# Per-block scale of the quantised activations: immediates in tensor_scalar against constant columns in tensor_tensor

## The chip, the cores and the metric

The kernel runs on 1 core of one Trainium2 chip. The metric is the device time in microseconds (us) of one execution. The engines are TensorE (PE in the profile), VectorE (DVE), ScalarE (ACT), GpSimd (POOL) and SyncE (SP), which here only issues transfers.

## The reference, cut to what matters

The program computes two layers on x of 8 x 512 x 256 (float32). The first layer, in which the change lies, is a layer norm followed by a state-space block and a quantised feed-forward block, both added to x:

```python
xn = _layernorm(x, axis=-1)
x = x + _L0_attn_ref(xn, ...) + _L0_ffn_ref(xn, w_gate, w_up, w_down)

def fp4_quant_dequant(x):                 # blocks of 16 along the last dim
    scale = jnp.max(jnp.abs(xb), axis=-1, keepdims=True) / 6.0
    scale = jnp.maximum(scale, jnp.float32(1e-12))
    xn = xb / scale
    idx = jnp.searchsorted(_MID, jnp.abs(xn))
    q = _GRID[idx] * jnp.sign(xn) * scale

gate = fp4_linear(x, w_gate); y = fp4_linear(x, w_up)
return fp4_linear(jax.nn.silu(gate) * y, w_down)

def step(h, inp):                         # state-space block, 512 steps
    dA = jnp.exp(d_t[:, :, None] * A[None])
    h = dA * h + (d_t * u_t)[:, :, None] * B_t[:, None, :]
    y_t = jnp.einsum('bdn,bn->bd', h, C_t)
```

The second layer (block-sparse attention, and two rounds of local attention with a feed-forward part) follows and is not touched.

## The kernel before, in words

Four stages run one after the other: the quantisation of the weights (to about 60 us), the state-space stage `mamba_and_fp4_ffn` (about 60 to 1530 us), block-sparse attention, and the local attention layers (from about 2160 us). Each engine has its own program, written out by hand; its order is the order in the code, and semaphores tie the engines together.

In the state-space stage one batch of 512 rows is one iteration, and it has 32 steps s. Each step handles two of the 16 states for 128 of the 512 channels. POOL multiplies `hb` = `bcB` * `du` (L540) for a step; ACT writes the decay `ps_dA` (L780, L782); DVE runs the scan over both (`tensor_tensor_scan`, L633) and multiplies the result by `bcC` into `hb` (L644, semaphore `weighed`); PE adds that into `ps_y` (L988). ACT may write the next but one `ps_dA` only once L644 has read the one before it. Between L633 and L644 of a step DVE runs what else is due in it. POOL works up to 8 steps ahead (a ring of 8 `hb` buffers) and is otherwise held only by its inputs.

The quantisation of activations is cut into three parts (`fp4_part`), placed in three steps in a row. Part 0 finds the largest magnitude of each block (L119), makes `scale` (L120), its reciprocal `inv` (L121), and corrects it by 1 - 2^-24 (L122). Part 1 multiplies by `inv` and makes the rounding constant in `work` (L125 to L127), part 2 rounds by adding and subtracting it (L129, L130). Every instruction of a part but the last waits for the one before it by a semaphore. POOL multiplies by `scale` afterwards (`scale_blocks`, L107).

In one batch part 0 runs five times: for `h` (the hidden rows, 704 values or 44 blocks per partition) in steps 3, 21, 25 and 29, called rows 0, 1, 2 and 3 below (tables `HIDDEN`), and for the next batch's `xn` (1024 values, 64 blocks) in step 13 (`XQ`). That makes 32 and 8 in the whole stage. In steps 1, 2, 4 and 6 PE also sums the output rows of the batch before it.

The stage's constants are set by POOL at its start, and DVE, ACT and PE wait for that count in `s_zero`.

Of the kernel before, what the change touches and what calls it, by code (L numbers as in the profile page):

```python
# [7 lines left out]
ALU = mybir.AluOpType  # L8
# [6 lines left out]
P = 128  # L15
# [54 lines left out]
def bc(ap, shape):  # L70
    return ap.broadcast_to(shape)
# [28 lines left out]
FP4_STEPS = 8  # L100
# [8 lines left out]

def fp4_part(dve, st, rows, blk, work, p, n, part):

    g = n // 16
    amax, scale, inv = blk[0:p, 0, 0:g], blk[0:p, 1, 0:g], blk[0:p, 2, 0:g]
    w = work[0:p, 0:n]
    blocks = rows.rearrange("p (g e) -> p g e", e=16)
    if part == 0:
        st.link(dve.tensor_reduce(amax, blocks, AX.X, ALU.max, apply_absolute_value=True))  # L119
        st.link(dve.tensor_scalar(scale, amax, 1.0 / 6.0, 1e-12, ALU.mult, ALU.max))  # L120
        st.link(dve.reciprocal(inv, scale))  # L121
        return st.done(dve.tensor_scalar(inv, inv, 1.0 - 2.0 ** -24, None, ALU.mult))  # L122
    if part == 1:
        dve.wait_ge(st.s, st.at(st.k))
        st.link(dve.tensor_tensor(blocks, blocks, bc(inv.unsqueeze(2), [p, g, 16]), ALU.mult))  # L125
        st.link(dve.tensor_scalar(w.bitcast(U32), rows.bitcast(U32), EXPONENT, None, ALU.bitwise_and))
        return st.done(dve.tensor_scalar(w, w, 1.0, 1.5 * 2.0 ** 22, ALU.max, ALU.mult))  # L127
    dve.wait_ge(st.s, st.at(st.k))
    st.link(dve.tensor_tensor(rows, rows, w, ALU.add))  # L129
    return dve.tensor_tensor(rows, rows, w, ALU.subtract)  # L130
# [85 lines left out]
def mamba_and_fp4_ffn(nc, io, W, x1_dram, bc_dram, NB):  # L216
# [6 lines left out]
    T, D, DI, NS, R, I = 512, 256, 512, 16, 16, 704  # L223
    TT, DC, IC = T // P, D // P, DI // P
# [11 lines left out]
    HIDDEN = [3, 21, 25, 29]  # L236
# [6 lines left out]
    XQ, TURN_XQ, TAKE_XQ = 13, 30, 31  # L243
# [12 lines left out]
    with ExitStack() as ctx:  # L256
        sb = lambda n, s, d=F32: ctx.enter_context(nc.sbuf_tensor(n, s, d))
        sems = []

        def S(name, per):  # L260
            sems.append(Sem(ctx, nc, name, per))
            return sems[-1]
# [10 lines left out]
        mhalf = sb("mhalf", [P, TT])  # L273
        eps = sb("eps", [P, TT])
        tick = sb("tick", [P, 1])


        xn = sb("xn", [P, TT, D])
# [19 lines left out]
        blk_x = sb("blk_x", [P, 3, TT * D // 16])  # L298
        blk_h = sb("blk_h", [P, 2, 3, I // 16])
        work = sb("work", [P, TT * D])  # L300
# [12 lines left out]
        s_zero = ctx.enter_context(nc.semaphore("a_zeroed"))  # L313
        s_aneg = ctx.enter_context(nc.semaphore("a_negA"))
        x_in = S("a_x_in", 16)
        xr_in = S("a_xr_in", 16)
        x_steps = S("a_x_steps", TT + 1 + FP4_STEPS)
        h_steps = S("a_h_steps", TT * FP4_STEPS)
        mv_ready = S("a_mv", TT)
        g_steps = S("a_g_steps", 2)  # L320
        xn_ready = S("a_xn", TT)
# [57 lines left out]
        def landed(s):  # L379

            return 16 * (s // ROWS + 1)

        def unit(s):
            return divmod(s, GROUPS)
# [88 lines left out]
        def _(pool):  # L473
# [3 lines left out]
            pool.memset(eps[:, :], LN_EPS).then_inc(s_zero, 1)  # L477
            pool.memset(xin[:, :, 0:3], 0.0).then_inc(s_zero, 1)
            pool.memset(nought[:, :], 0.0).then_inc(s_zero, 1)
            pool.wait_ge(s_zero, 6)  # L480

            def prepare(n, s):
                if s == STATS:
# [73 lines left out]
        @block.vector  # L557
        def _(dve):
            xs, hs = Steps(x_steps, dve), Steps(h_steps, dve)
            dve.wait_ge(s_w, 16 * 7)  # L560
            dve.wait_ge(s_zero, 6)
            dve.wait_ge(s_aneg, 1)
            for c in range(IC):
                dve.tensor_scalar(diag_d[:, c, :], W["ident"][:, :], cols[:, 2, c:c + 1], None, ALU.mult)\
                    .then_inc(s_aneg, 1)
                for j in range(4):
                    dve.tensor_scalar(diag_c[:, c, j, :], W["ident"][:, :], conv_w[:, c, j:j + 1], None, ALU.mult)\
                        .then_inc(s_aneg, 1)
            dve.tensor_scalar(a_neg[:, :, :], a_neg[:, :, :], -1.0, None, ALU.mult).then_inc(s_aneg, 1)

            def prepare(n, s):
                if s == STATS:
                    xs.turn(n)

                    dve.wait_ge(x_in.s, x_in.at(n, 16))
                    dve.wait_ge(xn_ready.s, xn_ready.at(n, 0))
                    for t in range(TT):
                        xs.done(dve.bn_stats(stats[:, t, :], xn[:, t, :]))
                    dve.wait_ge(xs.s, xs.at(TT))
                    xs.done(dve.memset(tick[:, :], 0.0))  # L580
                    for t in range(TT):
                        dve.bn_aggr(mv[:, t, :], stats[:, t, :]).then_inc(mv_ready.s, 1)
                if XQ <= s < XQ + 3:
                    rows = xn[:, :, :].rearrange("p t d -> p (t d)")
                    if s == XQ:
                        dve.wait_ge(xn_ready.s, xn_ready.at(n, TT))
                        dve.wait_ge(xn_turned.s, xn_turned.at(n, DC))
                    last = fp4_part(dve, xs, rows, blk_x, work, P, TT * D, s - XQ)
                    if s == XQ + 2:
                        last.then_inc(xg_ready.s, 1)  # L590

            def gate_y(b, c):
                dve.wait_ge(summed.s, summed.at(b, (c + 1) * GROUPS))
                dve.wait_ge(sz_ready.s, sz_ready.at(b, c + 1))
                dve.wait_ge(x1_sum.s, x1_sum.at(b, 0))
                dve.tensor_tensor(y[:, c, :], ps_y[:, :], z[:, c, :], ALU.mult).then_inc(y_ready.s, 1)

            def ffn(b, s, prev):
                for t in range(TT):
                    if HIDDEN[t] <= s < HIDDEN[t] + 3:  # L600
                        rows, blk = h[:, t % 2, :], blk_h[:, t % 2, :, :]
                        if s == HIDDEN[t]:
                            if t == 0:
                                hs.turn(b)
                            dve.wait_ge(sg_ready.s, sg_ready.at(b, t + 1))
                            dve.wait_ge(gated.s, gated.at(b, 2 * t + 2))
                            if t:
                                dve.wait_ge(h_turned.s, h_turned.at(b, 2 * t - 2))
                            elif prev:
                                dve.wait_ge(h_turned.s, h_turned.at(b - 1, 2 * TT - 2))  # L610
                            dve.tensor_tensor(rows.rearrange("p (a n) -> p a n", a=2), ps_p[:, :, 0:HALF],
                                              sg[:, :].rearrange("p (a n) -> p a n", a=2), ALU.mult).then_inc(h_ready.s, 1)
                            dve.wait_ge(h_ready.s, h_ready.at(b, t + 1))
                        last = fp4_part(dve, hs, rows, blk, work, P, I, s - HIDDEN[t])
                        if s == HIDDEN[t] + 2:
                            last.then_inc(hg_ready.s, 1)

            def first(n):
                for s in range(SCANS):
                    prepare(n, s)  # L620

            def tail(b):
                gate_y(b, IC - 1)

            def body(b, prev, more):
                flat = lambda ap: ap.rearrange("p n t -> p (n t)")

                for s in range(SCANS):
                    c, g = unit(s)
                    dve.wait_ge(dA_ready.s, dA_ready.at(b, s + 1))  # L630
                    dve.wait_ge(dBu_ready.s, dBu_ready.at(b, s + 1))
                    tile, h_all = hb[:, s % RING, :, :], dA[:, s % 2, :, :]
                    dve.tensor_tensor_scan(flat(h_all), flat(h_all), flat(tile), 0.0, ALU.mult, ALU.add)\  # L633
                        .then_inc(scanned.s, 1)
                    if g == 0 and c:
                        gate_y(b, c - 1)
                    if s == 0 and prev:
                        gate_y(b - 1, IC - 1)
                    ffn(b, s, prev)
                    if more:  # L640
                        prepare(b + 1, s)
                    dve.wait_ge(scanned.s, scanned.at(b, s + 1))
                    dve.wait_ge(c_in[s % ROWS].s, c_in[s % ROWS].at(b, landed(s)))
                    dve.tensor_tensor(tile, h_all, bcC[:, s % ROWS, :, :], ALU.mult).then_inc(weighed.s, 1)  # L644

            batches(dve, first, body, tail)

        @block.scalar
        def _(act):
            act.wait_ge(s_w, 16 * 7)  # L650
            act.activation(a_neg[:, :, :], a_neg[:, :, :], ACT.Exp).then_inc(s_aneg, 1)
            act.wait_ge(s_aneg, 2 + 5 * IC)
            act.wait_ge(s_zero, 6)

            def softplus(m, c):

# [145 lines left out]
        @block.tensor  # L802
        def _(pe):
            pe.wait_ge(s_w, 16 * 7)
            pe.wait_ge(s_zero, 6)
            pe.wait_ge(s_aneg, 2 + 5 * IC)

            def turn(src, k):
# [1538 lines left out]
```

## Time and profile before

| | us |
|---|---|
| median of 3 runs | 3789.05 |
| lowest, highest | 3785.77, 3795.94 |
| the profiled execution, its time | 3792.24 |
| its span, first to last instruction | 3790.1 |
| state-space stage within it, about | 1470 |
| one batch of that stage in steady state, about | 177 |

Over the whole span PE is busy 87%, DVE 67%, ACT 45%, POOL 42%. These shares mix four stages with different limits, so the state-space stage is read apart from the rest, and in it one steady batch. Times are from the start of the span. A busy span is what the profiler reports for an instruction; where an instruction has been started and cannot go on, that time is inside its duration and not in the idle time before it. So the duration of one instruction of fixed size, at its smallest and at its largest, is the thing to compare.

### The profile page before, as it was taken

To read this page: it belongs to the slowest core of one execution; us is meant where nothing else is said; L and a number is where in the kernel's file an instruction comes from. 1 tells how busy PE (TensorE), PEld (TensorE's weight loads), DVE (VectorE), ACT (ScalarE), POOL (GpSimd) and SP (SyncE) were. 2 spreads that over 40 slices of the span, in tenths; PEclk is the share of its full clock that TensorE was granted. 3 is DMA by queue.
4 is the path that set the end of the run, shared out by engine and by line. 5 is a ranking of instruction groups with operands and counts; after the bars stand their busy time and mean duration, and the time that the engine had idled before them with its cause. 6 is when DMAs were issued, how large, how long until landed. Compare 5 with 4: busy or idle time off the path is not lost. (4 is left out here: it accounts for less than half of the span.)

```text
span 3790.1 us, 50238 instructions
## 1 busy us (share of the span) xinstructions
PE 3296.6 (87%) x16236; PEld 1902.6 (50%) x16236; DVE 2545.5 (67%) x3554; ACT 1706.7 (45%) x4102; POOL 1579.5 (42%) x974
## 2 busy tenths in 40 slices
PE   2788898989798987699999769999999689999998
PEld 1334343444444343466666535655665355656665
DVE  5597989888888889376777545555555255555553
ACT  1564656556473743265566423333333133333332
POOL 1556465655555554000000044444554265555552
PEclk8899999999898998899999979999999799999999
DMA  1565556556565655100110010000000200000000
GB/s 47 192 207 191 198 198 209 200 189 213 181 222 183 208 195 180 53 23 22 33 33 17 28 61 17 17 17 17 17 17 12 69 17 22 22 22 22 22 17 17
DMA packets 146654, 343.30 MB, mean 91 GB/s; under 512 B 14898, under 2 KB 78470, under 8 KB 146582
## 3 DMA queue, kind: packets, MB, share of 16 engines
q1 hardware_dynamic: 138134, 334.02, 26.4%
q10 hardware_dynamic: 8448, 8.39, 0.7%
q8 instruction: 37, 0.61, 0.1%
q14 instruction: 35, 0.29, 0.0%
HBM read 320.87 MB, written 21.50 MB: 90 GB/s over the span
## 5 line engine op out<-in xcount | busy, mean ns | idle before, releaser
L988 PE MATMUL ps_y<-hb,ident 128*128 128x512 f32 x1024 | 537.3, 654 | 160.1 <-DVE hb L644 159.9
L633 DVE TENSOR_TENSOR_SCAN ps_dA<-ps_dA,hb 128x1024 f32<-128x1024 f32 x256 | 585.8, 2288 | 95.7 <-ACT ps_dA L782 65.7
L540 POOL TENSOR_TENSOR hb<-bcB,du 128x1024 f32<-128x1024 f32 x256 | 597.3, 2357 | 22.1 <-DMA bcB<-bc_scratch 14.4
L988 PEld LDWEIGHTS ps_y<-hb,ident 128*128 128x128 f32 x1024 | 194.1, 200 | 430.9 <-DVE hb L644 246.8
L1778 POOL TENSOR_TENSOR c_pr<-c_pr,c_inv 128x512 f32<-128x512 f32 (+1 forms) x256 | 232.6, 935 | 411.5 <-DVE c_inv L1890 409.5
L1348 ACT ACTIVATE b_pr<-b_ps_s,b_negmax 128x256 f32<-128x256 f32 (+1 forms) x512 | 263.8, 527 | 164.7 <-DVE b_negmax L1262 162.9
L2245 PE MATMUL c_ps_s<-c_hT,c_w 128*128 128x512 f32 x704 | 321.0, 603 | 17.2 <-DVE c_hid L1956 15.4
L2007 ACT ACTIVATE c_pr<-c_ps_s,c_negmax 128x256 f32<-128x256 f32 (+1 forms) x512 | 222.2, 446 | 246.4 <-DVE c_negmax L1885 246.4
L782 ACT ACTIVATE ps_dA<-delta,a_neg 128x511 f32<-128x511 f32 x512 | 329.7, 675 | 0.9
L644 DVE TENSOR_TENSOR hb<-ps_dA,bcC 128x1024 f32<-128x1024 f32 x256 | 312.0, 1219 | 5.3 <-issue 0.3
L1755 POOL TENSOR_TENSOR c_q_cos<-c_q_cos,c_q_sin 128x1024 f32<-128x1024 f32 x64 | 150.9, 2358 | 311.3 <-DVE c_q_sin L1864 311.3
L780 ACT ACTIVATE ps_dA<-nought 128x2 f32<-128x2 f32 x256 | 44.2, 173 | 491.3 <-DVE hb L644 490.6
L1262 DVE TENSOR_REDUCE b_negmax<-b_ps_s 128x2 f32<-128x512 f32 (+1 forms) x320 | 204.5, 683 | 71.9 <-PE b_ps_s L1419 70.9
L2095 PE MATMUL c_ps_s<-c_w_qkv,c_xT 128*128 128x512 f32 x512 | 241.1, 615 | 1.4 <-ACT c_xT L1980 1.4
L1885 DVE TENSOR_REDUCE c_negmax<-c_ps_s 128x2 f32<-128x512 f32 (+1 forms) x256 | 147.9, 620 | 127.7 <-PE c_ps_s L2132 127.3
L1206 POOL TENSOR_TENSOR b_xb<-b_xb,b_o_bias 128x1024 f32<-128x1024 f32 x8 | 18.8, 2348 | 497.4 <-DMA b_xb<-x_scratch 497.4
L2245 PEld LDWEIGHTS c_ps_s<-c_hT,c_w 128*128 128x128 f32 x704 | 129.6, 192 | 177.4 <-issue 147.8
L1433 PE MATMUL b_ps_t<-ident,b_pr 128*128 128x128 f32 x1280 | 189.6, 285 | 24.7 <-DVE b_pt L1284 12.8
L1956 DVE SCALAR_TENSOR_TENSOR c_hid<-c_ps_s,c_b_cols,c_gl 128x512 f32<-128x512 f32 x96 | 70.5, 745 | 196.3 <-ACT c_gl L2060 177.0
L1761 POOL TENSOR_TENSOR c_rn<-c_ssc,c_mhalf 128x16 f32<-128x16 f32 x64 | 186.5, 2913 | 31.7 <-DVE c_ssc L1874 31.2
L1433 PEld LDWEIGHTS b_ps_t<-ident,b_pr 128*128 128x128 f32 x1280 | 136.7, 142 | 113.9 <-DVE b_pt L1284 55.7
L1986 ACT ACTIVATE c_sq<-c_ps_s 128x512 f32<-128x512 f32 x128 | 69.5, 594 | 256.3 <-PE c_ps_s L2095 256.3
(234 smaller groups left out, 6405.2 us busy)
## 6 DMA issues: line engine op xcount, KB each, us to landing
bcB<-bc_scratch SPq DMA_DIRECT2D x256, 512.0 KB, 4.8
bcC<-bc_scratch SPq DMA_DIRECT2D x256, 512.0 KB, 4.0
c_x<-stream_scratch SPq DMA_DIRECT2D x16, 512.0 KB, 4.9
c_xr<-stream_scratch SPq DMA_DIRECT2D x16, 512.0 KB, 4.3
xn<-in_x_dram SPq DMA_DIRECT2D x8, 512.0 KB, 5.0
xr<-in_x_dram SPq DMA_DIRECT2D x8, 512.0 KB, 6.2
x_scratch<-xr SPq DMA_DIRECT2D x8, 512.0 KB, 5.2
b_x<-x_scratch SPq DMA_DIRECT2D x8, 512.0 KB, 4.2
```

The source lines that it names most:

```text
L540: pool.tensor_tensor(hb[:, s % RING, :, :], bcB[:, s % ROWS, :, :], bc(du[:, c % 2, :].unsqueeze(1), [P, NG, T]), ALU.mult)\
L633: dve.tensor_tensor_scan(flat(h_all), flat(h_all), flat(tile), 0.0, ALU.mult, ALU.add)\
L644: dve.tensor_tensor(tile, h_all, bcC[:, s % ROWS, :, :], ALU.mult).then_inc(weighed.s, 1)
L782: last = act.activation(dA[:, s % 2, n, 1:], delta[:, c, 1:], ACT.Exp, scale=a_neg[:, c, g * NG + n:g * NG + n + 1])
L988: last = pe.matmul(ps_y[:, :], W["ident"][:, :], hb[:, r % RING, i, :], start=False, stop=(g == GROUPS - 1 and i == NG - 1))
L1262: dve.tensor_reduce(negmax[:, u, 0:heads], ps_s[:, u % 4, :].rearrange("p (h n) -> p h n", h=heads), AX.X, ALU.max, negate=True).then_inc( ...
L1348: last = act.activation(pr[:, u % 8, cols], ps_s[:, u % 4, cols], ACT.Exp, bias=negmax[:, u, i:i + 1], accum_out=den[:, qt, h:h + 1])
L1433: last = pe.transpose(ps_t[:, u % 2, k * P:(k + 1) * P], pr[:, u % 8, k * P:(k + 1) * P], W["ident"][:, :])
L1778: pool.tensor_tensor(rows, rows, bc(inv[:, u, :].unsqueeze(2), [P, 2, w]), ALU.mult)\
L2007: last = act.activation(pr[:, u % 6, i * w:(i + 1) * w], ps_s[:, u % 4, i * w:(i + 1) * w], ACT.Exp, bias=negmax[:, u, i:i + 1], accum_out ...
L2095: last = pe.matmul(ps_s[:, pair(t) + a, :], xT[:, k, t * P:(t + 1) * P], w_qkv[:, k, a * INNER:(a + 1) * INNER], start=(k == 0), stop=(k = ...
L2245: last = pe.matmul(ps_s[:, pair(j) + a, :], w_1[:, k, at:at + P], hT[:, k, :], start=(k == 0), stop=(k == DC - 1))
```

## The change

In part 0 of `fp4_part` the two `tensor_scalar` instructions become three `tensor_tensor` instructions. The one that did multiply and max with two immediates is split in two, since a `tensor_tensor` does one operation. The second operand is one column of a new tile `cst` (128 x 3), read with step 0 over the 44 or 64 blocks. POOL sets the three columns at the start of the stage. The weights' quantisation (`fp4_steps`) keeps its instructions.

```diff
-def fp4_part(dve, st, rows, blk, work, p, n, part):
+FP4_PART_STEPS = 9
+
+def fp4_part(dve, st, rows, blk, work, cst, p, n, part):
...
     if part == 0:
+        sixth, least, under = (bc(cst[0:p, i:i + 1], [p, g]) for i in range(3))
         st.link(dve.tensor_reduce(amax, blocks, AX.X, ALU.max, apply_absolute_value=True))
-        st.link(dve.tensor_scalar(scale, amax, 1.0 / 6.0, 1e-12, ALU.mult, ALU.max))
+        st.link(dve.tensor_tensor(scale, amax, sixth, ALU.mult))
+        st.link(dve.tensor_tensor(scale, scale, least, ALU.max))
         st.link(dve.reciprocal(inv, scale))
-        return st.done(dve.tensor_scalar(inv, inv, 1.0 - 2.0 ** -24, None, ALU.mult))
+        return st.done(dve.tensor_tensor(inv, inv, under, ALU.mult))
...
+        cst = sb("cst", [P, 3])
...
-            pool.wait_ge(s_zero, 6)
+            for i, value in enumerate((1.0 / 6.0, 1e-12, 1.0 - 2.0 ** -24)):
+                pool.memset(cst[:, i:i + 1], value).then_inc(s_zero, 1)
+            pool.wait_ge(s_zero, 9)
```

On DVE, in step 3 of a batch (row block 0 of `h`), this stood before, with a scan at either end:

```order
L633 SCALAR_TENSOR_TENSOR ps_dA<-ps_dA,hb 128x1024
L611 TENSOR_TENSOR h<-ps_p,sg 128x704
L119 TENSOR_REDUCE blk_h<-h 128x44
L120 TENSOR_SCALAR blk_h<-blk_h 128x44
L121 RECIPROCAL blk_h<-blk_h 128x44
L122 TENSOR_SCALAR blk_h<-blk_h 128x44
L644 TENSOR_TENSOR hb<-ps_dA,bcC 128x1024
```

and this stands there now (the lines are those of the changed kernel):

```order
L642 SCALAR_TENSOR_TENSOR ps_dA<-ps_dA,hb 128x1024
L620 TENSOR_TENSOR h<-ps_p,sg 128x704
L124 TENSOR_REDUCE blk_h<-h 128x44
L125 TENSOR_TENSOR blk_h<-blk_h,cst 128x44
L126 TENSOR_TENSOR blk_h<-blk_h,cst 128x44
L127 RECIPROCAL blk_h<-blk_h 128x44
L128 TENSOR_TENSOR blk_h<-blk_h,cst 128x44
L653 TENSOR_TENSOR hb<-ps_dA,bcC 128x1024
```

Between the reduction and the multiplication by `bcC` there are four instructions in place of three, three of them with two operands in SBUF; nothing else is moved, on DVE or on another engine. The same holds for the other part 0s.

## Rows read from the trace of the kernel before

**Rows 1.** Busy time by window: window, length, engines' busy (instructions), clock, DMA share, GB/s.
```profile
651.00:828.00 177.00, 151.24 (x410) 75.17 (x409) 155.41 (x127) 100.64 (x171) 97.65 (x53) 0.94 0.59 199
```

**Rows 2.** Waits, 651 to 828 us: waiter <- releaser: total us, times, longest.
```profile
PE ps_y L988 <- DVE hb L644: 16.8, 9, 4.6
...
ACT ps_dA L780 <- DVE hb L644: 59.2, 21, 13.4
```

**Rows 3.** Groups by line, DVE: operation, tiles, shapes, count, busy us, mean ns.
```profile
L120 DVE TENSOR_SCALAR blk_h<-blk_h 128x44 f32<-128x44 f32 x32 | 42.2, 1318 | 1.1
...
L122 DVE TENSOR_SCALAR blk_h<-blk_h 128x44 f32<-128x44 f32 x32 | 21.6, 674 | 1.1
...
L122 DVE TENSOR_SCALAR blk_x<-blk_x 128x64 f32<-128x64 f32 x8 | 12.0, 1500 | 0.3
L120 DVE TENSOR_SCALAR blk_x<-blk_x 128x64 f32<-128x64 f32 x8 | 11.8, 1470 | 0.3
```

**Rows 4.** One tile's instructions: duration in ns, smallest/median/largest, first and last start.
```profile
L120 DVE TENSOR_SCALAR blk_h<-blk_h x32: 186/514/5120, 149.6 to 1498.2; 128x44 f32<-128x44 f32 x32
...
L122 DVE TENSOR_SCALAR blk_h<-blk_h x32: 186/187/1803, 150.4 to 1498.9; 128x44 f32<-128x44 f32 x32
L125 DVE TENSOR_TENSOR h<-h,blk_h x32: 867/872/2066, 154.2 to 1502.7; 128x704 f32<-128x704 f32 x32
...
L1874 DVE TENSOR_TENSOR c_ssc<-c_ss,c_tiny x64: 174/651/1383, 2207.3 to 3675.4; 128x16 f32<-128x16 f32 x64
```

**Rows 5.** Timeline, local attention: start, length in us, engine, line, operation, tiles.
```profile
2471.57 1.91 POOL L1768 TENSOR_TENSOR c_qr<-c_q_cos,c_rn 128x1024 f32<-128x1024 f32 x1
...
2472.86 0.65 DVE L1874 TENSOR_TENSOR c_ssc<-c_ss,c_tiny 128x16 f32<-128x16 f32 x1
```

**Rows 6.** Timeline, first batch, step 4: POOL and DVE.
```profile
153.16 2.35 POOL L540 TENSOR_TENSOR hb<-bcB,du 128x1024 f32<-128x1024 f32 x1
...
154.19 2.07 DVE L125 TENSOR_TENSOR h<-h,blk_h 128x704 f32<-128x704 f32 x1
...
155.46 3.00 POOL L540 TENSOR_TENSOR hb<-bcB,du 128x1024 f32<-128x1024 f32 x1
```

**Rows 7.** Timeline, a steady batch, step 3 (row block 0 of h): POOL and DVE.
```profile
668.04 6.96 POOL L540 TENSOR_TENSOR hb<-bcB,du 128x1024 f32<-128x1024 f32 x3
...
669.93 5.12 DVE L120 TENSOR_SCALAR blk_h<-blk_h 128x44 f32<-128x44 f32 x1
...
675.08 0.43 DVE L121 RECIPROCAL blk_h<-blk_h 128x44 f32<-128x44 f32 x1
675.08 1.26 POOL L532 TENSOR_TENSOR du<-delta,u 128x512 f32<-128x512 f32 x1
675.54 0.84 DVE L122 TENSOR_SCALAR blk_h<-blk_h 128x44 f32<-128x44 f32 x1
...
676.58 2.36 POOL L540 TENSOR_TENSOR hb<-bcB,du 128x1024 f32<-128x1024 f32 x1 [0.23 <-POOL du L532]
```

**Rows 8.** Timeline, the same batch, step 13 (xn): POOL and DVE.
```profile
726.25 4.67 POOL L540 TENSOR_TENSOR hb<-bcB,du 128x1024 f32<-128x1024 f32 x2
...
726.99 1.68 DVE L120 TENSOR_SCALAR blk_x<-blk_x 128x64 f32<-128x64 f32 x1
...
728.70 0.55 DVE L121 RECIPROCAL blk_x<-blk_x 128x64 f32<-128x64 f32 x1
...
729.29 1.69 DVE L122 TENSOR_SCALAR blk_x<-blk_x 128x64 f32<-128x64 f32 x1
```

**Rows 9.** Timeline, the same batch, step 25 (row block 2 of h): POOL and DVE.
```profile
786.98 4.65 POOL L540 TENSOR_TENSOR hb<-bcB,du 128x1024 f32<-128x1024 f32 x2
...
788.86 0.52 DVE L120 TENSOR_SCALAR blk_h<-blk_h 128x44 f32<-128x44 f32 x1
...
789.87 1.80 DVE L122 TENSOR_SCALAR blk_h<-blk_h 128x44 f32<-128x44 f32 x1
```

**Rows 10.** Timeline, the same batch: TensorE where it is released late.
```profile
685.07 0.74 PE L952 MATMUL ps_t<-xr,ident 128*128 128x256 f32 x2 [3.59 <-ACT hqT L732]
...
732.16 1.98 PE L988 MATMUL ps_y<-hb,ident 128*128 128x512 f32 x4 [0.31 <-DVE hb L644]
```

More of the change, by code:

```diff
@@ L316, in mamba_and_fp4_ffn @@
         xr_in = S("a_xr_in", 16)
-        x_steps = S("a_x_steps", TT + 1 + FP4_STEPS)
-        h_steps = S("a_h_steps", TT * FP4_STEPS)
+        x_steps = S("a_x_steps", TT + 1 + FP4_PART_STEPS)
+        h_steps = S("a_h_steps", TT * FP4_PART_STEPS)
         mv_ready = S("a_mv", TT)
@@ L560, in _ @@
             dve.wait_ge(s_w, 16 * 7)
-            dve.wait_ge(s_zero, 6)
+            dve.wait_ge(s_zero, 9)
             dve.wait_ge(s_aneg, 1)
@@ L587, in prepare @@
                         dve.wait_ge(xn_turned.s, xn_turned.at(n, DC))
-                    last = fp4_part(dve, xs, rows, blk_x, work, P, TT * D, s - XQ)
+                    last = fp4_part(dve, xs, rows, blk_x, work, cst, P, TT * D, s - XQ)
                     if s == XQ + 2:
@@ L613, in ffn @@
                             dve.wait_ge(h_ready.s, h_ready.at(b, t + 1))
-                        last = fp4_part(dve, hs, rows, blk, work, P, I, s - HIDDEN[t])
+                        last = fp4_part(dve, hs, rows, blk, work, cst, P, I, s - HIDDEN[t])
                         if s == HIDDEN[t] + 2:
@@ L652, in _ @@
             act.wait_ge(s_aneg, 2 + 5 * IC)
-            act.wait_ge(s_zero, 6)
+            act.wait_ge(s_zero, 9)
             def softplus(m, c):
@@ L804, in _ @@
             pe.wait_ge(s_w, 16 * 7)
-            pe.wait_ge(s_zero, 6)
+            pe.wait_ge(s_zero, 9)
             pe.wait_ge(s_aneg, 2 + 5 * IC)
```

## The prediction

> **What bounds the kernel now.** I read the busy time by window first, then the waits, then one steady batch on the timeline.
>
> By window, one steady batch (177 us) has DVE busy 155.4 us and PE 151.2 us, while ACT is at 100.6 and POOL at 97.7 [rows 1]. Two engines are near full, so the question is which is late where. The waits answer it: PE's longest total is 16.8 us for DVE's multiplication L644, and ACT waits 59.2 us for the same instruction [rows 2]. DVE's own order, from scan to scan, is the chain for most steps.
>
> Two places of the batch show how a delay on DVE reaches the others. At 685.07 PE starts a long stretch of work after an idle time of 3.59 us that ends with ACT's copy of `hqT`; that copy stands in ACT's order behind the decay for which ACT waits on L644. From there PE works without a gap of note up to 732.16, where it waits 0.31 us for L644 [rows 10]. So time lost by DVE in step 3 moves the whole PE stretch, and time lost in step 13 is on the path at once. In steps 21, 25 and 29 DVE has no idle time that another engine's own work sets. I therefore count every delay of part 0 in full.
>
> **What is wrong with the two instructions today.** `tensor_scalar` on 44 values takes 186 ns at its smallest and 5120 ns at its largest [rows 4]. The size is always the same, so the rest is waiting inside the instruction. The groups sum to 42.2 + 21.6 + 12.0 + 11.8 = 87.6 us [rows 3]. The timeline names the partner: L120 of 669.93 ends at 675.05, which is when the third of three POOL multiplications ends (668.04 + 6.96 = 675.00), and L122 of 675.54 ends at 676.38, with POOL's L532 (675.08 + 1.26 = 676.34) [rows 7]. DVE and POOL exclude each other here. Everything depends on whether a `tensor_tensor` with both operands in SBUF is excluded too.
>
> **Does tensor_tensor wait as well?** Two kinds of row say yes. In the local attention stage L1874 is a `tensor_tensor` on 16 values with a tile of constants as second operand: it takes 174 ns at its smallest, 1383 at its largest [rows 4]. One of them starts at 2472.86, inside POOL's L1768, and ends at 2473.51; POOL's instruction ends at 2473.48 [rows 5]. In this stage L125, with 704 values, takes 872 ns as a rule and 2066 once [rows 4], at 154.19, inside POOL's L540 that ends at 155.51; and the POOL instruction behind it takes 3.00 us in place of 2.35 [rows 6], so POOL was held in its turn. No row has a two-operand DVE instruction in SBUF running beside a POOL one at its small price. What no row shows is an operand of step 0, a single column; L125's second operand repeats each value 16 times, and that is the nearest.
>
> The Trainium skill says it too, in "SBUF — State Buffer", section "SBUF: two separate sides": the port pair is taken for a whole instruction by a DVE instruction in a two-port mode, or by one with two SBUF inputs against a GpSimd one that reads SBUF. By this rule, which speaks against the change, the sum is the one below; by the view that only two-port modes take the pair it would be that of the first rival. The rows above side with the rule.
>
> **Prices.** Free of POOL, `tensor_tensor` takes 174 ns for 16 values and 872 for 704 [rows 4]: 1.015 ns for each more, so 202 ns for 44 and 223 for 64. Between linked instructions there are 34 ns (675.05 to 675.08, [rows 7]). Where POOL is out of the way, part 0 gets longer by one instruction and its gap (0.24 us) and by 2 x 16 ns: **0.27 us**. A waiting `tensor_tensor` ends about 0.06 us after POOL's for 44 values, 0.08 for 64.
>
> **Part by part, with POOL where it stands today.** The new third instruction matters more by what it meets than by its length.
>
> *Row block 0, step 3* [rows 7]. The first multiplication ends at 675.06, as L120 does. The maximum starts at 675.10, just after POOL's L532 (675.08), and waits till 676.40. The reciprocal (0.43) ends at 676.87. The correction starts at 676.90, inside POOL's next L540 (676.58 + 2.36 = 678.94), and ends at 679.00 in place of 676.38: **2.6 us**. POOL's next instruction waits for DVE, so nothing more follows. The pattern stands in six batches, the second to the seventh (L120 of 3.4 or 5.1 us in each): 15.6 us.
>
> *xn, step 13* [rows 8]. The first ends at 728.67, between two POOL instructions; the maximum starts at 728.70 inside the second, which ends at 726.25 + 4.67 = 730.92, and ends at 731.00. Reciprocal 0.55 and correction 0.22 with their gaps: 731.84, in place of 730.98: 0.87 us, seven times, 6.1 us. (The eighth lies before the first scan; 0.3 at most.)
>
> *Row block 2, step 25* [rows 9]. In the same way the maximum waits from 789.41 to 791.69 (POOL ends at 786.98 + 4.65 = 791.63), and the correction ends at 792.38 in place of 791.67: 0.71 us, seven times, 5.0 us.
>
> *The rest*: L122's median is 187 ns [rows 4], so in most part 0s POOL is idle behind L120. Row blocks 1 and 3 of all batches and 0 and 2 of the last: 18 x 0.27 = 4.9 us. Row block 0 of the first batch: 0 to 2.3 us, since the three instructions of part 1 behind it wait for POOL today and would wait less; I take 1.
>
> *The three memsets* on POOL at the start lie under the loading of the weights: nothing.
>
> The sum is 15.6 + 6.1 + 5.0 + 4.9 + 1.0 = 32.6 us. The profiled execution (span 3790.1, time 3792.24) would go to 3822.7 and 3824.8. Its time is 3.2 us above the median of the runs; on the median the forecast is 3789.05 + 33 = **3822 us**, 0.9% slower.
>
> **The rivals.**
>
> *The new operation does not wait* (its step-0 operand, or its single element per cycle, keeps it off the shared resource). Then 87.6 us [rows 3] become 96 x 0.202 + 24 x 0.223 + 40 x 0.034 = 26.1 us; the gain of 61.5 us gives 3728. For it speaks only that no row has this operand; against it L1874 and L125. 7%.
>
> *DVE slips in between.* The maximum comes 34 ns behind the first multiplication, and may run before POOL's next instruction has really begun. In step 3 the margin is 0.02 us. If it wins there alone, the maximum ends at 675.30, the correction waits for L532 and ends at 676.40 as today, and the sum is 33 - 15.6 = 17, so 3806. 15%. If it wins in steps 13 and 25 too, the later wait swallows the extra instruction there, and only the 18 x 0.27 is left with some tenths: 3794, no change that can be told. Against the second speaks that POOL's instruction had been waiting with its start on record 0.1 us before. 10%.
>
> *The delays are hidden*: PE's stretch from 685 or ACT turns out to be bound by something else than DVE. Then 3789 to 3792. The wait of 0.31 us at 732.16 [rows 10] leaves little room. 6%.
>
> **How the numbers follow.** Forecast 62%, first rival 7%, second 15% and 10%, third 6%. Around the forecast, phases may move: DVE's later times put other part 0s under a POOL instruction (5 of the 18 free ones by 2.36 us would be 12 us more), so the upper end is 3835. The lower end takes in both forms of slipping in and most of the hidden case, and reaches 3790; below it lie the 7% and part of the 6%, above it some 8%. A measurement tells about 0.3%, 11 us, from no change. From the cases: faster 0.07; same 0.10 + 0.06 = 0.16; slower 0.62 + 0.15 = 0.77.
>
> **What would show it.** In the changed kernel's profile the three `blk_h<-blk_h,cst` groups should have smallest durations near 202 ns and largest in the thousands, the maximum and the correction each ending with a POOL instruction. Step 3 should have waits in all three, and a batch should last some 181.5 us in place of 177. If the three groups stand at 0.2 us throughout, the first rival is right, and my reading of L1874 wrong. If the maximum stays at 0.2 us where POOL is busy, DVE slips in. If the waits are there and the batch is not longer, the path was read wrong.

## The result and the profile after

| | time, median of runs (us) | lowest to highest |
|---|---|---|
| before, same chip | 3791.08 | 3785.77 to 3795.94 |
| changed kernel | 3825.58 | 3818.32 to 3827.98 |

The ratio is 1.0088, 95% interval 1.0068 to 1.0108: 34.5 us slower, where the forecast had 33. The profiled execution of the changed kernel is the fastest of its four (3818.32 us, span 3816.4), so its trace shows 26.3 us of the 34.5 against the span of before (3790.1). The other three runs of the changed kernel are 7 to 10 us longer than the profiled one.

From the page of the changed kernel, the busy time of each engine with its share and its count of instructions.

```profile
PE 3297.9 (86%) x16236; PEld 1901.0 (50%) x16236; DVE 2569.5 (67%) x3594; ACT 1705.5 (45%) x4102; POOL 1577.7 (41%) x977
```

DVE has 40 instructions and 24.0 us of busy time more than before (x3554, 2545.5 us). Forty instructions of 0.2 us would be 8 us; most of the rest is waiting inside the three operations. One steady batch and its largest wait of PE, columns as in [rows 1] and [rows 2]:

```profile
671.00:852.00 181.00, 154.19 (x414) 76.89 (x415) 159.25 (x133) 101.01 (x173) 98.64 (x55) 0.93 0.58 197
```

```profile
PE ps_y L997 <- DVE hb L653: 20.2, 10, 5.3
```

DVE is busy 159.2 us of 181 in place of 155.4 of 177, and PE waits 20.2 us for DVE's multiplication (L653 here, L644 before) in place of 16.8. From first scan to last the state-space stage takes 1402.38 us in place of 1372.14: 30.2 more. The rest of the program is 3.9 us shorter in this execution. The block-sparse stage alone, which the change does not touch, takes 614.5 us here and 618.8 in the trace of before, and 614.5 to 625.3 in the traces of the kernels below, so that the time of a single trace differs by some microseconds for this alone.

The new instructions, by tile and line: smallest, median and largest duration in ns, first and last start in us.

```profile
L125 DVE TENSOR_TENSOR blk_h<-blk_h,cst x32: 203/522/5108, 149.0 to 1527.9; 128x44 f32<-128x44 f32 x32
L126 DVE TENSOR_TENSOR blk_h<-blk_h,cst x32: 203/206/2265, 149.3 to 1528.2; 128x44 f32<-128x44 f32 x32
...
L128 DVE TENSOR_TENSOR blk_h<-blk_h,cst x32: 203/203/2076, 150.9 to 1528.9; 128x44 f32<-128x44 f32 x32
```

```profile
L125 DVE TENSOR_TENSOR blk_x<-blk_x,cst x8: 225/1672/1687, 84.0 to 1284.8; 128x64 f32<-128x64 f32 x8
L126 DVE TENSOR_TENSOR blk_x<-blk_x,cst x8: 226/2272/2278, 84.2 to 1286.6; 128x64 f32<-128x64 f32 x8
```

The free prices are 203 and 225 ns (202 and 223 were estimated), the largest are in the thousands: a `tensor_tensor` whose second operand is one repeated column waits for POOL too. Step 3 of one steady batch, DVE and then POOL; it answers to [rows 7]:

```profile
502.11 5.11 DVE L125 TENSOR_TENSOR blk_h<-blk_h,cst 128x44 f32<-128x44 f32 x1
507.25 1.30 DVE L126 TENSOR_TENSOR blk_h<-blk_h,cst 128x44 f32<-128x44 f32 x1
...
509.06 2.07 DVE L128 TENSOR_TENSOR blk_h<-blk_h,cst 128x44 f32<-128x44 f32 x1
```

```profile
500.20 6.95 POOL L549 TENSOR_TENSOR hb<-bcB,du 128x1024 f32<-128x1024 f32 x3
507.23 1.26 POOL L541 TENSOR_TENSOR du<-delta,u 128x512 f32<-128x512 f32 x1
508.73 2.34 POOL L549 TENSOR_TENSOR hb<-bcB,du 128x1024 f32<-128x1024 f32 x1 [0.23 <-POOL du L541]
```

The first multiplication ends with the third of POOL's three (507.22 and 507.15), the maximum with the multiplication of `du` (508.55 and 508.49), the correction with the next one (511.13 and 511.07). All three wait, and the wait of the correction is what makes the 2.6 us of the forecast. Note the start times 507.25 and 507.23: the maximum comes 0.02 us after POOL. Step 13 and step 25 went as written too. The multiplication and the maximum of xn, against [rows 8]:

```profile
561.73 1.67 DVE L125 TENSOR_TENSOR blk_x<-blk_x,cst 128x64 f32<-128x64 f32 x1
563.44 2.27 DVE L126 TENSOR_TENSOR blk_x<-blk_x,cst 128x64 f32<-128x64 f32 x1
```

### The profile page after: what moved, and what is told of

It is laid out like the page before. It is cut to its first block and busy times, and to the rows that moved or that the text cites. A ratio compares the mean times of both kernels' runs of the same rounds, so it can differ in the third digit from the quotient of the medians.

```text
span 3816.4 us, 50503 instructions
## 1 busy us (share of the span) xinstructions
PE 3297.9 (86%) x16236; PEld 1901.0 (50%) x16236; DVE 2569.5 (67%) x3594; ACT 1705.5 (45%) x4102; POOL 1577.7 (41%) x977
## 5 line engine op out<-in xcount | busy, mean ns | idle before, releaser
L653 DVE TENSOR_TENSOR hb<-ps_dA,bcC 128x1024 f32<-128x1024 f32 x256 | 312.0, 1219 | 5.1
```

## The experiments

My theory: the cost is one more instruction in a chain that stands next to POOL's instructions, each of which can hold it for a whole POOL instruction; the kind of the operation does not matter. Rivals: the cost is the kind (`tensor_tensor` with two reads waits where `tensor_scalar` would not), or it is what PE does with the delay. The kernels were run in two sets, each with the kernel before beside them, and each ratio goes by that one: it took 3794.13 us (3788.88 to 3799.7) beside `two_tt`, `split_ts` and `reduce_pairs`, and 3791.36 (3785.07 to 3798.3) beside `first_ts`, `first_tt`, `step3_kept` and `odd_rows`. "At step 3" and the like is the difference to the trace of before from the start of the batch's first scan to the scan behind that step.

### Each form by itself, beside a busy POOL

The kernel computes nothing of the reference. DVE runs seven forms of a 44-value operation with reciprocals between them, first alone, then while POOL runs linked multiplications of 1024 values, then while POOL runs them back to back.

```python
link(dve.tensor_scalar(dst[:, 0, 0:44], a, 0.5, None, ALU.mult))
link(dve.reciprocal(dst[:, 1, 0:44], a))
link(dve.tensor_tensor(dst[:, 2, 0:44], a, bc(cst[:, 0:1], [P, 44]), ALU.mult))
...
link(dve.tensor_reduce(dst[:, 5, 0:44], pairs[:, 0:44, :], AX.X, ALU.mult))
...
link(dve.tensor_scalar(dst[:, 6, 0:44], odd[:, :, 0:4], 0.5, None, ALU.mult))
```

> Leaves the whole computation out (the output is set to zero) and measures the disputed cost by itself: DVE runs seven forms on 44 values, one after the other with a reciprocal between them, first with POOL idle, then beside POOL multiplications of 1024 values of which each waits for the one before, then beside POOL multiplications that are all ready. The forms: tensor_scalar with an immediate; tensor_tensor with a single column read with step 0; tensor_tensor with a full second operand; tensor_tensor with its second operand in PSUM; tensor_reduce over pairs; tensor_scalar with input rows of 4 out of 5 written flat; tensor_scalar with its input in PSUM. Theory (two SBUF operands are excluded by POOL as tensor_scalar is): with POOL idle about 190 to 270 ns each; beside POOL the first three reach 0.5 to 2.4 us, the column like the full operand, while those with PSUM and the tensor_reduce keep their price. Rival (the single column is free): the second form stays near 0.2 us beside POOL. Beside POOL instructions that are all ready, the first three may wait for more than one of them, so beyond 2.4 us. For the tensor_scalar with rows of 4 out of 5 no theory says which.

Durations in ns (smallest, median, largest), alone and beside the linked POOL instructions (`spaced`), which fill the stretch (53.12 us for 22 of them):

```profile
L142 DVE TENSOR_SCALAR alone<-src x2: 186/187/188, 4.7 to 9.7; 128x44 f32<-128x44 f32 x2
...
L144 DVE TENSOR_TENSOR alone<-src,cst x2: 203/203/203, 5.4 to 10.3; 128x44 f32<-128x44 f32 x2
```

```profile
L142 DVE TENSOR_SCALAR spaced<-src x5: 1486/1489/2369, 14.7 to 54.3; 128x44 f32<-128x44 f32 x5
L143 DVE RECIPROCAL spaced<-src x5: 427/428/428, 17.1 to 55.8; 128x44 f32<-128x44 f32 x5
L144 DVE TENSOR_TENSOR spaced<-src,cst x5: 1937/1937/1941, 17.6 to 56.3; 128x44 f32<-128x44 f32 x5
...
L146 DVE TENSOR_TENSOR spaced<-src,zero x5: 1920/1923/1923, 20.0 to 58.7; 128x44 f32<-128x44 f32 x5
...
L148 DVE TENSOR_TENSOR spaced<-src,psc x5: 199/199/200, 22.4 to 61.1; 128x44 f32<-128x44 f32 x5
...
L150 DVE TENSOR_REDUCE spaced<-pairs x5: 245/245/245, 23.1 to 61.8; 128x44 f32<-128x88 f32 x5
...
L152 DVE TENSOR_SCALAR spaced<-odd x5: 199/199/200, 23.9 to 62.5; 128x44 f32<-128x44 f32 x5
...
L154 DVE TENSOR_SCALAR spaced<-psc x5: 203/203/203, 24.5 to 63.2; 128x44 f32<-128x44 f32 x5
```

Three forms wait: `tensor_scalar` on plain SBUF tiles, and `tensor_tensor` with two SBUF operands, whether the second is a repeated column (L144) or a whole tile (L146). The first rival of the prediction is gone. Five do not: the reciprocal, `tensor_reduce` over pairs, `tensor_tensor` or `tensor_scalar` with an operand in PSUM (`psc`), and `tensor_scalar` whose source is 11 rows of 4 with a pitch of 5 (`odd`) and whose destination is 44 in a row. That last form takes 199 ns in place of 187, and never waits. Beside POOL instructions that are all ready (`queued`) the medians of the three that wait are 1250, 1819 and 1800 ns, so none waited for more than the one POOL instruction in hand, of 2.34 us; the expectation had held more than one to be possible. The Trainium skill, "VectorE: DVE Perf Modes", section "What auto-detection actually checks", has it that the two-port mode wants source and destination in SBUF with outermost sizes both even or equal; 11 against 44 is neither, so L142 and L152 agree with it, and L154 with the words on SBUF.

### One wait point fewer

The changed kernel without the maximum; it leaves out the floor of 1e-12 under the scale.

```diff
         st.link(dve.tensor_tensor(scale, amax, sixth, ALU.mult))
-        st.link(dve.tensor_tensor(scale, scale, least, ALU.max))
         st.link(dve.reciprocal(inv, scale))
```

> Leaves out the floor of 1e-12 (the maximum), so part 0 has again three instructions behind the reduction's result: tensor_tensor, reciprocal, tensor_tensor. Theory (it is the third instruction that costs, the kind costs nothing): the waits of before, 16 to 28 ns more for each of 80 instructions, about 1.5 us: 3792, no change. Rival (the tensor_tensor kind itself waits longer or holds POOL up): half of the loss or more stays, 3808 or above.

Measured: 3798.26 us, ratio 1.001 (1.0 to 1.002). With two `tensor_tensor` in the places of the two `tensor_scalar`, the time is nearly that of before: 4.1 us above it, where 1.5 were expected. Its stage is 7.6 us longer, of which 4.6 come in the first batch, where a single first multiplication waited 8.28 us (340 ns in the first batch of before):

```profile
L125 DVE TENSOR_TENSOR blk_h<-blk_h,cst x32: 203/534/8283, 149.9 to 1506.1; 128x44 f32<-128x44 f32 x32
```

In the six steady batches step 3 differs by -0.01 to +0.13 us. So the kind alone, without the third instruction, costs next to nothing in the steady batches.

### The third instruction, of the old kind

The kernel before, with its first `tensor_scalar` parted in two.

```diff
-        st.link(dve.tensor_scalar(scale, amax, 1.0 / 6.0, 1e-12, ALU.mult, ALU.max))
+        st.link(dve.tensor_scalar(scale, amax, 1.0 / 6.0, None, ALU.mult))
+        st.link(dve.tensor_scalar(scale, scale, 1e-12, None, ALU.max))
```

> The kernel before with its first tensor_scalar split in two (mult, then max, both with an immediate); no tensor_tensor is added. Theory (the third instruction and what it meets): step 3 again 2.6 us later in six batches, step 13 and step 25 by 0.8 and 0.7 us in seven, the others 0.22 us: some 31 us, 3821. Rival (the kind): under 10 us.

Measured: 3807.55 us, ratio 1.0042 (1.0028 to 1.0056): 13.4 us, half of what the theory wanted and more than the rival allowed. Both missed. Steps 13 and 25 cost nearly what they cost in the changed kernel (0.77 to 0.82 and 0.66 to 0.83 us), but step 3 of the six steady batches only 0.02 to 0.04. In the first batch a first operation waited 8.28 us as in `two_tt`, and 4.1 us of it are left behind step 8; so some 4 of the 15.9 us by which this trace's stage is longer have nothing to do with the theory. The timeline of step 3, DVE then POOL:

```profile
500.88 5.10 DVE L120 TENSOR_SCALAR blk_h<-blk_h 128x44 f32<-128x44 f32 x1
506.02 0.19 DVE L121 TENSOR_SCALAR blk_h<-blk_h 128x44 f32<-128x44 f32 x1
...
506.70 0.66 DVE L123 TENSOR_SCALAR blk_h<-blk_h 128x44 f32<-128x44 f32 x1
```

```profile
506.02 1.30 POOL L533 TENSOR_TENSOR du<-delta,u 128x512 f32<-128x512 f32 x1
```

Here the maximum starts at 506.02, level with POOL, and lasts 0.19: it slipped in, and POOL's instruction takes 1.30 us in place of 1.26. This is the second rival of the prediction, in its form "at step 3 alone", which had 17 us for the kernel changed. In the changed kernel the maximum started 0.02 us after POOL's and waited 1.3. What differs is the first multiplication. `tensor_scalar` is 16 ns shorter than `tensor_tensor` once POOL lets it run (187 against 203 ns, L142 and L144 above), and by my reading those 16 ns decide who is first. That was an idea from two timelines; the next three runs put it to the test.

### Which of the three must be short

`first_ts` is the changed kernel with `tensor_scalar` for the first operation alone, `first_tt` the reverse.

```diff
-        st.link(dve.tensor_tensor(scale, amax, sixth, ALU.mult))
+        st.link(dve.tensor_scalar(scale, amax, 1.0 / 6.0, None, ALU.mult))
```

> The kernel changed, with only its first multiplication put back to a tensor_scalar (mult alone); maximum and correction stay tensor_tensor. Theory (a race of some 20 ns): in step 3 the tensor_scalar ends about 18 ns earlier than the tensor_tensor did, the maximum asks before POOL's multiplication of du has begun, runs in 0.2 us, and the correction ends with that POOL instruction as before; so the 2.6 us of step 3 are gone in six batches and what is left is steps 13, 25 and the free ones, as when both operations were tensor_scalar: about 3808. Rival (a maximum by tensor_tensor always waits there): about 3825, as the kernel changed.

```diff
-        st.link(dve.tensor_tensor(scale, scale, least, ALU.max))
+        st.link(dve.tensor_scalar(scale, scale, 1e-12, None, ALU.max))
...
-        return st.done(dve.tensor_tensor(inv, inv, under, ALU.mult))
+        return st.done(dve.tensor_scalar(inv, inv, 1.0 - 2.0 ** -24, None, ALU.mult))
```

> The reverse: the first multiplication is a tensor_tensor, the maximum and the correction are tensor_scalar with immediates. Theory (the race): the maximum asks 18 ns too late in step 3 and waits for POOL's multiplication of du, the correction for the next one; 2.6 us in six batches, about 3823. Rival (the kind of the maximum decides): about 3808.

Measured: 3810.09 us, ratio 1.0046 (1.0032 to 1.006), for the first, and 3818.78, 1.007 (1.0047 to 1.0092), for the second. One changed operation out of three takes step 3 from +2.6 to +0.06 us (0.19 in one batch); putting the other two back to `tensor_scalar` does not help (+2.54, 2.67 in one). The second was expected at 3823. The two kernels differ by 8.7 us, and by 7.2 in the stage, though step 3 alone makes 14.9 us between them in six batches: 4.2 of that go back in the stretch of PE that is shown below under "Forms that do not wait". Step 3 of `first_ts`, DVE and POOL:

```profile
499.01 5.09 DVE L125 TENSOR_SCALAR blk_h<-blk_h 128x44 f32<-128x44 f32 x1
504.14 0.20 DVE L126 TENSOR_TENSOR blk_h<-blk_h,cst 128x44 f32<-128x44 f32 x1
```

```profile
504.14 1.32 POOL L541 TENSOR_TENSOR du<-delta,u 128x512 f32<-128x512 f32 x1
```

And of `first_tt`:

```profile
502.43 5.11 DVE L125 TENSOR_TENSOR blk_h<-blk_h,cst 128x44 f32<-128x44 f32 x1
507.58 1.29 DVE L126 TENSOR_SCALAR blk_h<-blk_h 128x44 f32<-128x44 f32 x1
```

```profile
507.56 1.26 POOL L541 TENSOR_TENSOR du<-delta,u 128x512 f32<-128x512 f32 x1
```

A `tensor_tensor` slips in (L126 of the first), a `tensor_scalar` comes too late (L126 of the second), so the kind of the one that waits does not decide. In the six steady batches of `split_ts` and `first_ts` the maximum starts 0 to 3 ns ahead of POOL's instruction and slips in; in those of `first_tt` and the changed kernel it starts 14 to 20 ns behind it and waits: twelve cases of each, without an exception. What sets the start is the operation ahead, which ends 0.04 us after POOL's as a `tensor_scalar` and 0.06 after it as a `tensor_tensor`. Its length and its kind change together in these runs, and none changes its length alone. That its kind is not enough shows in the first batch of `first_ts`: there the maximum stands behind a `tensor_scalar` too, starts 0.12 us behind a POOL instruction, and waits (1.03 us).

### The third instruction taken out of step 3 alone

The changed kernel, with the multiplication and the maximum in one `tensor_scalar` for row block 0 of h, the one of step 3.

```diff
...
+        if one:
+            st.link(dve.tensor_scalar(scale, amax, 1.0 / 6.0, 1e-12, ALU.mult, ALU.max))
+        else:
+            st.link(dve.tensor_tensor(scale, amax, sixth, ALU.mult))
+            st.link(dve.tensor_tensor(scale, scale, least, ALU.max))
...
```

> The kernel changed, except that row block 0 of h (step 3) has mult and max in one tensor_scalar again; its correction stays a tensor_tensor. Theory: step 3 costs 2.6 us in six of the batches and up to 2.3 in the first, so 15.6 to 18 us less than the kernel changed: 3808 to 3810. Rival (the places share the loss, or what step 3 gives back is lost at PE): over 3818.

Measured: 3807.51 us, ratio 1.0041 (1.0028 to 1.0054). Step 3 is back at +0.01 to +0.14 in five of the six steady batches, and at -3.63 in one, and the whole lies 18.3 us under the changed kernel (34.5 less 16.2, each against its own before), where 6 x 2.6 + 2.3 = 17.9 was to be removed. That one batch shows something else. Its first operation got in as soon as the POOL instruction in hand had ended, where those of the other five steady batches wait for one or two more (DVE, then POOL):

```profile
856.11 0.50 DVE L126 TENSOR_SCALAR blk_h<-blk_h 128x44 f32<-128x44 f32 x1
```

```profile
854.22 6.98 POOL L552 TENSOR_TENSOR hb<-bcB,du 128x1024 f32<-128x1024 f32 x3
```

It lasts 0.50 us. The same instruction of step 3 lasts 5.07 to 5.12 us in four other batches, with POOL's instructions around its start at the same distance to within 0.04 us.

### Forms that do not wait

If the waits are the cost, a part 0 without them gains on the kernel before. `reduce_pairs` keeps the three operations, and makes each a `tensor_reduce` over pairs of a value and a constant beside it, which POOL's three memsets write once.

```diff
...
+        pair = [cst[0:p, i, 0:g, :] for i in range(3)]
+        st.link(dve.tensor_reduce(pair[0][:, :, 0], blocks, AX.X, ALU.max, apply_absolute_value=True))
+        st.link(dve.tensor_reduce(pair[1][:, :, 0], pair[0], AX.X, ALU.mult))
+        st.link(dve.tensor_reduce(scale, pair[1], AX.X, ALU.max))
+        st.link(dve.reciprocal(pair[2][:, :, 0], scale))
+        return st.done(dve.tensor_reduce(inv, pair[2], AX.X, ALU.mult))
...
```

> Computes the same values as the kernel changed, but each constant is laid beside its operand in pairs, and mult and max are done by tensor_reduce over a pair, which has one operand and is not seen to wait for POOL. Theory: a tensor_reduce of 88 values costs about 0.27 us and of 128 about 0.31 (from 886 ns for 704 values and 1208 for 1024), so the 120 new instructions take 33 us in place of the 87.6 us of before, and since DVE is on the path all of it shows: about 53 us less than before, 3738. Rival (part 0's time is not on the path in full): the gain is well under 40 us. Rival (any DVE instruction waits for POOL here): no gain, or slower than the kernel changed.

`odd_rows` uses for h the two `tensor_scalar` of before, reading from 11 rows of 4 with a pitch of 5, and for xn the pairs.

```diff
...
+        four = lambda ap: ap.rearrange("p (a b) -> p a b", b=4)
+        st.link(dve.tensor_reduce(odd[0:p, 0, :, 0:4], rows.rearrange("p (a b e) -> p a b e", b=4, e=16), AX.X,
+                                  ALU.max, apply_absolute_value=True))
+        st.link(dve.tensor_scalar(scale, odd[0:p, 0, :, 0:4], 1.0 / 6.0, 1e-12, ALU.mult, ALU.max))
+        st.link(dve.reciprocal(odd[0:p, 1, :, 0:4], four(scale)))
+        return st.done(dve.tensor_scalar(inv, odd[0:p, 1, :, 0:4], 1.0 - 2.0 ** -24, None, ALU.mult))
...
```

> Computes the same values. For h, amax and the reciprocal lie in 11 rows of 4 in a pitch of 5, and the two tensor_scalar of before read them so and write 44 flat values; in the probe that form took 199 ns beside a busy POOL. For xn the constants stay in pairs with tensor_reduce. Theory: each of the 32 part 0s of h has one instruction less than with the pairs and saves 3 x 245 + 34 - 2 x 199 = 0.37 us, 12 us in all: 3745 against 3757. Rival (with the waits gone, the next bound is PE or ACT): within 4 us of 3757.

Measured: 3757.12 us, ratio 0.9903 (0.9886 to 0.992), and 3746.67, ratio 0.9882 (0.9865 to 0.9899). The second is the fastest of all: 44.7 us under before, 79 under the changed kernel. It was expected at 3745, 12 us under `reduce_pairs`, and in the traces its stage is 11.9 us shorter than that one's. The maximum in `reduce_pairs`, and the first `tensor_scalar` of `odd_rows`:

```profile
L126 DVE TENSOR_REDUCE blk_h<-cst x32: 244/245/246, 150.9 to 1467.9; 128x44 f32<-128x88 f32 x32
```

```profile
L125 DVE TENSOR_SCALAR blk_h<-odd x32: 198/199/200, 148.5 to 1454.0; 128x44 f32<-128x44 f32 x32
```

None of the 32 waits, nor do the others of this work in either kernel (largest: 246, 201 and, for xn, 288 ns). Many of them stand beside a busy POOL: of the 64 `tensor_scalar` of `odd_rows`, 45 overlap an instruction of POOL. What part 0 spends on this work falls from 87.6 us [rows 3] to 2 x 6.4 + 3 x 2.3 = 19.7 us in `odd_rows`: 68 less. Only 43.5 of it reached the stage, and `reduce_pairs` was expected at 3738, 53 to 56 us faster, and gave 37. Most of the rest came back one part later. In `odd_rows`, from the groups by line (busy us, mean ns):

```profile
L138 DVE TENSOR_TENSOR h<-h,blk_h 128x704 f32<-128x704 f32 x32 | 36.9, 1153 | 0.0
L140 DVE TENSOR_SCALAR work<-work 128x704 f32<-128x704 f32 x32 | 31.0, 968 | 1.1
...
L139 DVE TENSOR_SCALAR work<-h 128x704 uint32<-128x704 uint32 x32 | 23.5, 734 | 1.1
```

The same three lines take 29.1, 17.8 and 18.9 us in the trace of before (L125, L127 and L126), so 25.6 us are waits that moved from part 0 to part 1, and 67.9 - 25.6 = 42.3, about the 43.5 of the stage. For `reduce_pairs` the same count gives 57.3 - 17.9 = 39.4, and its stage has 31.6. Where they fall shows in step 4 of a steady batch of `odd_rows`, DVE then POOL:

```profile
488.62 1.68 DVE L138 TENSOR_TENSOR h<-h,blk_h 128x704 f32<-128x704 f32 x1
490.33 1.48 DVE L139 TENSOR_SCALAR work<-h 128x704 uint32<-128x704 uint32 x1
491.84 2.54 DVE L140 TENSOR_SCALAR work<-work 128x704 f32<-128x704 f32 x1
```

```profile
484.89 4.66 POOL L557 TENSOR_TENSOR hb<-bcB,du 128x1024 f32<-128x1024 f32 x2
...
489.62 1.79 POOL L549 TENSOR_TENSOR du<-delta,u 128x512 f32<-128x512 f32 x1
...
491.65 2.35 POOL L557 TENSOR_TENSOR hb<-bcB,du 128x1024 f32<-128x1024 f32 x1 [0.23 <-POOL du L549]
```

Before, part 1 came when POOL's burst was over; now it comes 5.6 us earlier, into the burst, and its three instructions wait in turn (5.70 us, where with POOL idle they take 0.87 + 0.53 + 0.53 = 1.93). Step 3 gains 5.57 us in each steady batch. Of that 3.77 (5.70 - 1.93) go to the waits of step 4, and PE's long stretch starts 1.7 to 1.8 us earlier than before, counted from the batch's first scan. Behind step 8, 0.5 to 2.4 us are left. The start of the stretch in the same batch, before and then `odd_rows`:

```profile
508.66 1.22 PE L952 MATMUL ps_t<-xr,ident 128*128 128x256 f32 x2 [3.17 <-ACT hqT L732]
509.67 3.87 PE L954 MATMUL ps_t<-downT,hqT 128*128 128x256 f32 x12
```

```profile
497.83 1.22 PE L969 MATMUL ps_t<-xr,ident 128*128 128x256 f32 x2 [6.11 <-ACT hqT L749]
498.85 5.11 PE L971 MATMUL ps_t<-downT,hqT 128*128 128x256 f32 x12
```

PE starts after 6.11 us of idle time instead of 3.17, and its 12 matmuls take 5.11 us instead of 3.87. The mean granted clock of these fourteen matmuls is 0.71 before and 0.55 in `odd_rows`, that is, a larger share of them at 1.2 in place of 2.4 GHz. But this batch is the one where the two differ most. Over the six steady batches, us from the first of the fourteen to the end of the last, with the granted clock:

| | second | third | fourth | fifth | sixth | seventh |
|---|---|---|---|---|---|---|
| before | 6.34, 0.53 | 4.88, 0.71 | 5.17, 0.67 | 5.69, 0.60 | 6.08, 0.57 | 6.46, 0.52 |
| changed | 6.05, 0.57 | 5.17, 0.67 | 3.48, 1.00 | 6.47, 0.52 | 6.11, 0.56 | 5.12, 0.67 |
| `odd_rows` | 6.42, 0.53 | 6.13, 0.55 | 6.03, 0.57 | 5.92, 0.58 | 5.88, 0.58 | 5.86, 0.59 |

In all, `odd_rows` takes 1.6 us more than before here and `reduce_pairs` 1.5 us less, so this is a small part of what came back. Another 4.0 us come back in both kernels at step 16, 0.56 to 0.58 in each of the first seven batches: there DVE now waits 0.60 to 0.61 us (0.45 in the first) for PE's sum `ps_y` before it reads it, and at most 0.03 before.

## Why the prediction was right, step by step

**Does it wait?** Right, and now shown for the very operand (L144 against L146 in the kernel of single forms). The rows that the prediction leaned on had 16 and 704 values, and none a single column; the repeated column behaves as they do. The Trainium skill's rule in "SBUF — State Buffer", section "SBUF: two separate sides", named two SBUF inputs; L148, with one of the two in PSUM, does not wait, which agrees.

**The prices.** 203 and 225 ns against 202 and 223; 0.28 us measured for a free part 0 (step 29) against 0.27.

**Row block 0, step 3.** The prediction had 2.6 us in each of six batches, 15.6 in all. Measured: 2.69, 2.57, 2.57, 2.56, 2.58, 2.58, or 15.6. But the term hung on more than it said. It put the margin at 0.02 us and held the outcome for the likely one, and the runs show that an operation ahead that is 16 ns shorter, a `tensor_scalar`, turns it over. That the margin fell on this side was in part luck. For `split_ts` I then expected the waits of the changed kernel, having left that margin out of the sum: the same step failed there (31 us expected, 13.4 measured). The prediction's second rival was thus not wrong as a mechanism; it is what `split_ts`, `first_ts` and `step3_kept` measure (13.4, 18.7 and 16.2 us, against the 17 worked out, the last by another road). The agreement is rough: in the traces `split_ts` has 4.1 us from its first batch, and `step3_kept` gains 3.6 at step 3 of the one batch shown above.

**xn, step 13, and row block 2, step 25.** 0.85 to 0.87 us against 0.87; 0.70 to 0.87 (0.70 to 0.72 in five of the seven) against 0.71. Right. That the maximum would not slip in there either was right too.

**The first batch.** Taken at 1 us within 0 to 2.3; it was 2.31, the upper end. In the last batch step 3 cost 0.62 against 0.27.

**Every delay counted in full.** Nearly. The 30.2 us of the stage are 18.5 from step 3, 6.0 from step 13, 5.3 from step 25 in the first seven batches and 2.0 from step 29 in these, together 31.7; then -2.2 between step 3 and step 9, and 0.7 in all the rest. Of the part 0s that the prediction counted as free, those of step 29 cost what was forecast, and the eight of step 21 cost 0.8 us in place of 2.2. The -2.2 is the difference of the rows "before" and "changed" in the table above (-1.7 to +0.8 from batch to batch): the same fourteen matmuls take 3.48 us at a granted clock of 1.00 and 6.47 at 0.52. The prediction had no term for it, and I can't forecast it. A batch was to last 181.5 us, and the six steady ones last 179.7 to 181.9, 180.9 in the mean, against 176.8 before.

**The sum.** For the profiled execution 3822.7 us of span were forecast, and it has 3816.4: 2.3 of the difference are in the stage (30.2 against 32.6) and 3.9 in stages that the change does not touch. The median gives 34.5 against 33 (3825.58 us against 3822, since before has 3791.08 here in place of 3789.05). The agreement within 1.5 us is better than the working deserves, with runs that spread by 10 us.

**What stays open.** Why one DVE instruction that waits gets in at the first end of a POOL instruction, and another, of the same line and at the same distance, is passed over once, twice or, in `two_tt` and `split_ts`, for 8.3 us. In the kernel of single forms none was ever passed over, with POOL's instructions back to back and linked alike. One thing sets the places apart, in all nine traces of the whole program: of the waits of part 0, none was passed over where POOL's next instruction started after a gap (86 cases with one of 0.08 to 0.5 us, 172 with a longer one), and all 74 times that one was passed over, POOL's next instruction followed without a gap. It is not enough by itself, for in 111 other cases without a gap, and in 8 of the kernel of single forms, the waiting instruction got in. What decides among those was not settled. It is worth up to 4.6 us in the first batch of `two_tt`. Also open is how the loss of `reduce_pairs` from 39.4 to 31.6 us divides: 4.0 come back at step 16, PE's clock in the fourteen matmuls is not in it, and the rest is spread over several steps.

## What to carry to other kernels

Where two engines shut each other out for the length of an instruction, count the places at which a short chain can be shut out, not its busy time: a third operation of 0.2 us cost 2.6 us in one place and 0.28 in another, and a kernel with as many instructions as the changed one (`reduce_pairs`), but without these waits, was 37 us faster than before. Where an order between two engines is decided by a few hundredths of a microsecond, work out both outcomes, and let each experiment's expectation carry both. And a wait that is taken out of a chain may meet the same POOL instructions one part later: look at what then stands beside the burst before adding up the gain.

## What the runs showed of the hardware that I had not expected

- Behind a first operation of 187 ns (`tensor_scalar`) the next one runs in 0.19 us and the correction in 0.66; behind one of 203 (`tensor_tensor`) the next waits 1.3 and the correction 2.1.
- A `tensor_scalar` with the source in 11 rows of 4 (pitch 5) and the destination flat takes 199 ns and was never held by POOL, 45 times beside a busy POOL in `odd_rows` and 8 times among the single forms; plain, it takes 187 and lasted up to 5120 ns [rows 4], or 8276 in `split_ts`.
- `tensor_reduce` over pairs (245 ns for 44 values) does the work of a `tensor_tensor` with a constant, and did not wait for POOL once.
- POOL can start one or more further instructions while a DVE instruction waits (up to 8.3 us), but did so only where its next instruction followed without a gap; in the kernel of single forms it never did.
